# First two stages in one block with overlaid buffers; two buffers for the output weights, two groups per loop turn, exponentials head by head

## The chip, the cores and the metric

The kernel runs on one core of one Trainium2 chip. Its five engines (PE = TensorE, DVE = VectorE, ACT = ScalarE, POOL = GpSimd, SP = SyncE) run their own instruction streams and meet at semaphores. The metric is the device time of one execution, in microseconds (us).

## What is computed

Four adapter layers, each added to its input `x` (8 sequences of 128 tokens, 512 features, float32). The second is attention with 32 query heads and 8 key/value heads of size 128, rotary positions and rank-16 adapters that each sequence picks from 8.

```python
x = x + einsum('bsi,boi->bso', x, L0_weight[ids])                 # layer 0: a 512x512 weight per sequence
# layer 1, lora_linear(x, w, a, b) = x@w + (x@a[id])@b[id]
q, k = rope(lora_linear(x, wq, aq, bq)), rope(lora_linear(x, wk, ak, bk))
v    = lora_linear(x, wv, av, bv)
p    = softmax(where(causal & mask, q.k / sqrt(128), min))        # 4 query heads share a key head
x    = x + lora_linear((p @ v), wo, ao, bo)
x = x + ((x @ B[ids].T) @ A[ids].T)                               # layer 2, rank 16
x = x + x @ W.T + b + 2.0 * ((x @ lora_As[s]) @ lora_Bs[s])       # layer 3, rank 16
```

## The kernel before

Nearly every product is made of three matmuls: each float32 operand is split into a high part (rounded, by ACT) and a low part (the rest, by DVE or POOL), and PE adds hi*hi, hi*lo and lo*hi. The program is four blocks, one after the other; between two blocks all engines meet.

**Block 1** (layer 0, sequence by sequence, b = 0..7). SP loads the transposed input (256 KB), the weight of the sequence (1 MB, three buffers), `x` (256 KB) and the three `a` adapters (96 KB). ACT and DVE split them. PE makes the product (`product`, L282 to L284, 12 matmuls of 512 columns), transposes the sum with four float32 transposes (`turn_x1`, L294), multiplies by the `a` adapters (`adapters`, L306 to L308) and turns those (`turn_ax`, L318). POOL issues gathers of the `bk` and `bv` rows of the sequences into a DRAM tensor `bkv_sel` (L267, L268), from which SP later loads one block of rows with four DMAs (`load_rows`, L154).

**Block 2** (projections). 16 value units (L713 to L718: 12 matmuls of 512 columns and one for the adapters), 16 key units and 4 query units (`project`, L80 to L85), in five weight blocks. For each weight block SP loads 1 MB of weights and 1 MB of adapter rows, and ACT and DVE split them piece by piece. Value units are split and stored to DRAM by SP (L526, two DMAs for each unit, two buffers), key units are rotated by DVE and POOL and stored by SP (L531, two buffers). POOL issues gathers of `bq`, `ao`, `bo` and `l3b` rows. PE may run four units ahead of DVE (four PSUM banks).

**Block 3** (the loop). 8 groups of 4 heads, 8 slots (sequences) in each; the first and the last group are written out, the six between are a hardware loop (`over_heads`). Slot t is in order on PE: scores(t), 8 passes (L1079); queries for later (L80 to L85); turn(t-1), which transposes the probabilities as a product with an identity (L1088, L1089: eight float16 matmuls, high and low half); outputs(t-2) (L1111 to L1113, then L1120 and L1121); values(t-1) (L1097 to L1099). DVE: maxima of four heads (L1015), `ot_lo`, residual add, inverse row sums (L1032, L1034), rotation (L969, L973), `pt_lo`, `p_lo` (L1044). ACT: four exponentials (L889) after the last maximum, `pt_hi` (L872), `p_hi` (L905), `ot_hi` (L878) and the high parts of the next weights. POOL: the probabilities times the inverse sums (L944), rotation (L937), low parts of the query weights (L929). The output weights have one buffer: their high parts are made in slot 1 of their own group, two low parts by DVE (L984) and two by POOL (L954).

**Block 4** (layers 2 and 3) is not changed, but for the place of one buffer.

What sets the order around the change is the program text: each engine goes through its list in order and waits at semaphores, SP's list of DMAs included. Names and lines are in the functions below.

Of the kernel before, what the change touches and what calls it, by code (L numbers as in the profile page):

```python
# [7 lines left out]
P = 128  # L8
# [19 lines left out]
P_SCALE = 4096.0  # L28
# [3 lines left out]
def program(nc, x, xt, lora_ids, pos, attn_ids, slot_ids, mask, w0, wq, wk, wv, wo, a3, bq, bk, bv, ao, bo,  # L32
# [22 lines left out]
    bkv_sel = nc.dram_tensor("bkv_sel", (B, R, 2, KVH * D), F32, kind="Internal").ap()  # L55
# [10 lines left out]
    with whole:  # L66
# [24 lines left out]
        ident_r = sb(whole, "ident_r", [P, P], F32R)  # L91
        ident_h = sb(whole, "ident_h", [P, P], F16)
# [4 lines left out]

        row_gather = sb(whole, "row_gather", [2 * R, 2, P])

# [10 lines left out]

        attn = ExitStack()
# [3 lines left out]
        cos_t = sb(attn, "cos_t", [P, NT])  # L115
        sin_t = sb(attn, "sin_t", [P, NT])
# [4 lines left out]
        rope_cols = sb(attn, "rope_cols", [P, 3])  # L121

        blk_hi = [sb(attn, "blk_hi0", [P, KC, GW], F32R)]
        blk_lo = [sb(attn, "blk_lo0", [P, KC, GW], F32R)]
        blk_b = [sb(attn, "blk_b0", [P, PAIRS, GW], F32R)]
        VB = KVH * D // GW  # L130
        raw_w_in = sem(attn, "raw_w_in")
        raw_b_in = sem(attn, "raw_b_in")
        UNITS = B
        assert VB * GW == KVH * D and GW // D * 2 == UNITS and KC + PAIRS == UNITS

        def block_source(n):

            kind, j = ((1, n), (0, n - VB), (2, 0))[min(n // VB, 2)]
            return kind, j

        def load_block_w(dma, n):
            kind, j = block_source(n)
            dma.dma_start(raw_w[:, :, :], (wk, wv, wq)[kind][j]).then_inc(raw_w_in, 16)

        def load_block_b(dma, n):
            kind, j = block_source(n)
            cols = slice(j * GW, (j + 1) * GW)
            src = (bq_sel if kind == 2 else bkv_sel[:, :, kind, :])[:, :, cols]
            load_rows(dma, raw_b, src, raw_b_in)

        def load_rows(dma, pack, src, done):

            for quad in range(4):
                dma.dma_start(pack[32 * quad:32 * quad + 32, :, :], src.rearrange("(c two) r n -> (two r) c n", two=2)).then_inc(done, 16)  # L154


        with ExitStack() as c:
            RAW = 3
            w0_raw = [sb(c, f"w0_raw{i}", [P, KC, HID]) for i in range(RAW)]
            xt_raw = [sb(c, f"xt_raw{i}", [P, KC * T]) for i in range(RAW)]  # L160
            xt_hi = [sb(c, f"xt_hi{i}", [P, KC * T], F32R) for i in range(2)]
            xt_lo = [sb(c, f"xt_lo{i}", [P, KC * T], F32R) for i in range(2)]
            wt_hi = [sb(c, f"wt_hi{i}", [P, KC, HID], F32R) for i in range(2)]
            wt_lo = [sb(c, f"wt_lo{i}", [P, KC, HID], F32R) for i in range(2)]
            a_raw = sb(c, "a_raw", [P, B, KC, 3, R])
            a_hi = [sb(c, f"a_hi{i}", [P, KC, 3, R], F32R) for i in range(2)]
            a_lo = [sb(c, f"a_lo{i}", [P, KC, 3, R], F32R) for i in range(2)]
            axn = [sb(c, f"axn{i}", [P, 3, 4, 2, R], F32R) for i in range(2)]
            ps_y = [ps(c, f"ps_y{i}", [P, HID]) for i in range(2)]
            ps_x1 = [ps(c, f"ps_x1{i}", [P, KC, T]) for i in range(2)]  # L170
            ps_a = [ps(c, f"ps_a{i}", [P, 3, R]) for i in range(2)]
            ps_at = [ps(c, f"ps_at{i}", [P, 3, T]) for i in range(2)]
# [8 lines left out]
            gathered_kv = sem(c, "gathered_kv")  # L181
            raw_hi_done = sem(c, "raw_hi_done")
            raw_lo_done = sem(c, "raw_lo_done")
# [17 lines left out]
            axt_done = sem(c, "axt_done")  # L201

            def parts(b):
                return KC if b == 0 else 2

            def wt_parts(b, k):

                before = sum(parts(n) for n in range(b))
                return before + k * parts(b) // KC + 1

            with nc.Block() as block:
                @block.sync
                def _(sp):
                    sp.dma_start(id_rows[:, 0, :], lora_ids.rearrange("(a b) -> a b", a=1)).then_inc(lora_ids_in, 16)
                    sp.dma_start(xt_raw[0][:, :], xt[0]).then_inc(xt_in[0], 16)
                    sp.wait_ge(lora_ids_in, 16)
                    for b in range(B):
                        a = sp.value_load(id_rows[0:1, 0, b:b + 1], min_val=0, max_val=w0.shape[0] - 1)
                        if b >= RAW:

                            sp.wait_ge(wt_lo_done, wt_parts(b - RAW, KC - 1))
                            sp.wait_ge(xt_lo_done, b - RAW + 1)
                        src = w0[bass.DynSlice(a, 1)].rearrange("a p c o -> p (a c) o")
                        if b == 0:

                            for k in range(KC):
                                sp.dma_start(w0_raw[0][:, k, :], src[:, k, :]).then_inc(w0_first_in[k], 16)
                            sp.wait_ge(ids_in, 32)
                        else:
                            sp.dma_start(xt_raw[b % RAW][:, :], xt[b]).then_inc(xt_in[b % RAW], 16)  # L230
                            sp.dma_start(w0_raw[b % RAW][:, :, :], src).then_inc(w0_in[b % RAW], 16)
# [1302 lines left out]
```

## Time and profile before

| | us |
|---|---|
| median of three runs | 840.07 (839.33 to 841.19) |
| the profiled execution | 838.21, span of its instructions 836.4 |
| PE busy | 758.6 (91%) |
| DVE, ACT, POOL busy | 606.9, 360.9, 327.9 |
| mean granted clock of PE | 0.958 |
| PE's last projection starts / first scores of the loop / end of the loop | 218.54 / 225.78 / about 771 |

Busy shares are means over stages of different kinds; the stretches have to be read one by one. A matmul's duration includes its way through the array, so the distance between the starts of two is what it costs PE. Granted clock 1.0 is 2.4 GHz, 0.5 is 1.2 GHz.

### The profile page before, as it was taken

To read this page: it belongs to the slowest core of one execution; us is meant where nothing else is said; L and a number is where in the kernel's file an instruction comes from. 1 tells how busy PE (TensorE), PEld (TensorE's weight loads), DVE (VectorE), ACT (ScalarE), POOL (GpSimd) and SP (SyncE) were. 2 spreads that over 40 slices of the span, in tenths; PEclk is the share of its full clock that TensorE was granted. 3 is DMA by queue.
4 is the path that set the end of the run, shared out by engine and by line. 5 is a ranking of instruction groups with operands and counts; after the bars stand their busy time and mean duration, and the time that the engine had idled before them with its cause. 6 is when DMAs were issued, how large, how long until landed. Compare 5 with 4: busy or idle time off the path is not lost. (4 is left out here: it accounts for less than half of the span.)

```text
span 836.4 us, 13875 instructions
## 1 busy us (share of the span) xinstructions
PE 758.6 (91%) x4356; PEld 629.8 (75%) x4356; DVE 606.9 (73%) x1502; ACT 360.9 (43%) x967; POOL 327.9 (39%) x277
## 2 busy tenths in 40 slices
PE   3768849899689999999999999999999999987798
PEld 2657638687568888888888888888888888875586
DVE  3544266688488788789779778878877977854883
ACT  3545142311164464446446355446444644542550
POOL 3412620154274355337336426435524633510320
PEclk8878969999799999999999999999999999999799
DMA  8772977876205024122303303402412110610502
GB/s 296 274 225 72 281 235 190 230 244 189 65 7 170 1 64 139 39 63 67 108 17 108 113 0 97 141 0 63 138 38 63 63 38 27 136 17 4 127 17 85
DMA packets 61802, 88.92 MB, mean 106 GB/s; under 512 B 18550, under 2 KB 36118, under 8 KB 58054
## 3 DMA queue, kind: packets, MB, share of 16 engines
q1 hardware_dynamic: 59442, 81.92, 32.6%
q0 software_dynamic: 2176, 6.49, 2.6%
q8 instruction: 18, 0.29, 0.1%
q14 instruction: 18, 0.15, 0.1%
q10 hardware_dynamic: 148, 0.07, 0.0%
HBM read 73.50 MB, written 20.73 MB: 113 GB/s over the span
## 5 line engine op out<-in xcount | busy, mean ns | idle before, releaser
L944 POOL TENSOR_TENSOR prob<-prob,rinv 128x512 f32<-128x512 f32 x64 | 66.6, 1040 | 199.2 <-DVE rinv L1034 199.2
L889 ACT ACTIVATE prob<-sm,nmax 128x128 f32<-128x128 f32 x256 | 99.8, 391 | 80.3 <-DVE nmax L1015 80.3
L937 POOL TENSOR_TENSOR qt<-qc,qs 128x512 f32<-128x512 f32 x60 | 96.7, 1611 | 96.1 <-DVE qs L973 96.1
L1111 PE MATMUL ps_out<-wo_hi,ot_hi 128*128 128x512 f32 x256 | 106.4, 416 | 5.9 <-DVE ot_lo L992 3.7
L80 PE MATMUL ps_q<-x1t_hi,blk_hi 128*128 128x512 f32 x240 | 100.7, 420 | 0.0
L1113 PE MATMUL ps_out<-wo_hi,ot_lo 128*128 128x512 f32 x256 | 100.7, 393 | 0.0
L1112 PE MATMUL ps_out<-wo_lo,ot_hi 128*128 128x512 f32 x256 | 99.7, 390 | 0.0
L1015 DVE CUSTOM_DVE_ANT_0 sm<-ps_s,maskbias 128x128 f32<-128x128 f32 x256 | 58.7, 284 | 54.2 <-issue 54.1
L81 PE MATMUL ps_q<-x1t_lo,blk_hi 128*128 128x512 f32 x240 | 95.8, 399 | 0.0
L82 PE MATMUL ps_q<-x1t_hi,blk_lo 128*128 128x512 f32 x240 | 95.7, 399 | 0.0
L973 DVE TENSOR_TENSOR qs<-ps_q,sin_t 64x512 f32<-64x512 f32 x120 | 82.6, 688 | 3.7
L878 ACT ACTIVATE ot_hi<-ps_o 128x512 fp32r<-128x512 f32 x64 | 38.0, 594 | 105.6 <-PE ps_o L1099 105.4
L1079 PEld LDWEIGHTS ps_s<-kt,qt 128*128 128x128 f32 x512 | 67.6, 193 | 12.5 <-issue 7.0
L1079 PE MATMUL ps_s<-kt,qt 128*128 128x128 f32 x512 | 68.4, 277 | 6.8 <-PEq L514 6.8
L1044 DVE TENSOR_TENSOR p_lo<-prob,p_hi 128x512 f16<-128x512 f32 x64 | 59.8, 934 | 5.9 <-ACT p_hi L905 4.1
L1111 PEld LDWEIGHTS ps_out<-wo_hi,ot_hi 128*128 128x128 f32 x256 | 48.2, 188 | 15.4 <-DVE ot_lo L992 4.9
L872 ACT ACTIVATE pt_hi<-ps_t 128x512 fp32r<-128x512 f32 x64 | 38.2, 596 | 42.8 <-PE ps_t L1089 42.8
L1113 PEld LDWEIGHTS ps_out<-wo_hi,ot_lo 128*128 128x128 f32 x256 | 48.1, 188 | 11.2
L1112 PEld LDWEIGHTS ps_out<-wo_lo,ot_hi 128*128 128x128 f32 x256 | 48.4, 189 | 8.5
L82 PEld LDWEIGHTS ps_q<-x1t_hi,blk_lo 128*128 128x128 f32 x240 | 45.6, 190 | 10.9
L696 POOL TENSOR_TENSOR kr<-k_cos,k_sin 128x512 f32<-128x512 f32 x16 | 25.7, 1608 | 69.7 <-DVE k_sin L670 57.7
L905 ACT ACTIVATE p_hi<-prob 128x512 f16<-128x512 f32 x64 | 40.2, 628 | 29.1 <-POOL prob L944 28.8
(194 smaller groups left out, 1871.4 us busy)
## 6 DMA issues: line engine op xcount, KB each, us to landing
wo_raw<-in_wo SPq DMA_DIRECT2D x8, 1024.0 KB, 4.9
raw_w<-in_wq SPq DMA_DIRECT2D x8, 1024.0 KB, 5.3
w_raw<-in_w SPq DMA_DIRECT2D x7, 1024.0 KB, 9.7
raw_b<-bq_sel SPq DMA_DIRECT2D x56, 128.0 KB, 4.7
raw_b<-bkv_sel SPq DMA_DIRECT2D x16, 256.0 KB, 6.6
v_hi_d<-v_hi SPq DMA_DIRECT2D x16, 256.0 KB, 3.1
v_lo_d<-v_lo SPq DMA_DIRECT2D x16, 256.0 KB, 3.8
k_rot<-kr SPq DMA_DIRECT2D x16, 256.0 KB, 2.9
```

The costliest lines, as they stand in the source:

```text
L80: pe.matmul(bank[:, :], w_hi[:, k, cols], x1t_hi[:, k, tok], start=(k == 0), stop=False)
L81: pe.matmul(bank[:, :], w_hi[:, k, cols], x1t_lo[:, k, tok], start=False, stop=False)
L82: pe.matmul(bank[:, :], w_lo[:, k, cols], x1t_hi[:, k, tok], start=False, stop=False)
L889: e = act.activation(prob[i][:, h, :], sm[:, h, :], ACT.Exp, bias=nmax[i][:, h:h + 1], scale=-1.0, accum_out=rsum[i][:, h:h + 1])
L937: pool.tensor_tensor(qt[:, half, h, :], qc[:, :], qs[:, :], ALU.add).then_inc(q_done, 1)
L944: pool.tensor_tensor(prob[i][:, :, :], prob[i][:, :, :], rinv[i][:, :].unsqueeze(2).broadcast_to([P, G, T]), ALU.mult).then_inc(prob_done, 1)
L973: dve.tensor_tensor(qs[to:to + 64, :], ps_q[i][at:at + 64, :], sin_t[to:to + 64, tok], ALU.mult).then_inc(q_mult, 1)
L1044: dve.tensor_tensor(p_lo[:, :, :], prob[i][:, :, :], p_hi[:, :, :], ALU.subtract).then_inc(p_lo_done, 1)
L1079: mm = pe.matmul(ps_s[b % 2][:, h, :], qt[:, half, h, at:at + T], kt[:, b * T:(b + 1) * T], start=True, stop=True)
L1111: pe.matmul(ps_out[:, :], ot_hi[:, q], wo_hi[:, h, :], start=(h == 0), stop=False)
L1112: pe.matmul(ps_out[:, :], ot_hi[:, q], wo_lo[:, h, :], start=False, stop=False)
L1113: pe.matmul(ps_out[:, :], ot_lo[:, q], wo_hi[:, h, :], start=False, stop=(h == G - 1))
```

## The change

In the diff below, the loops over s are ACT's and PE's, `split_pieces` waits for all 32 DMAs of a block before the first piece of its rows, `load_a(b)` waits until the low part of the `a` adapters of sequence b-3 is made, and turn_ax(n) stands in the middle of values(n).

Blocks 1 and 2 become one block: in step s PE does value unit s-2, then product, adapters and first transposition of sequence s; key and query units follow. Most raw buffers lie over buffers that are used later. A table PIECES says in which step each quarter of a weight block is split. The gather into `bkv_sel` is gone: SP loads the adapter rows of a block directly with 32 DMAs. ACT issues the stores of the values. In the loop the float16 halves of the probabilities are gone, and PE transposes the float32 probabilities with four transposes, ahead of the queries. The output weights have two buffers and are split in slots 4 to 7 of the group before, all low parts on POOL; ACT makes each exponential after its own maximum; the loop turns three times over two groups.

```diff
+        PIECES = {1: [(0, "w", k) for k in range(KC)] + [(0, "b", 0)], 2: [(0, "b", 1)], 3: [(0, "b", 2), (0, "b", 3)],
+                  4: [(1, "b", 0), (1, "b", 1)], 5: [(1, "b", 2), (1, "b", 3)],
+                  7: [(1, "w", 0), (1, "w", 1)], 8: [(1, "w", 2), (1, "w", 3)],
+                  10: [(2, "b", 0)], 11: [(2, "w", 0)], 12: [(2, "w", 1)], 13: [(2, "w", 2)], 14: [(2, "w", 3)],
+                  15: [(2, "b", 1)], 16: [(2, "b", 2)], 17: [(2, "b", 3)]}
+        for k in range(KC):
+            PIECES[18 + k] = [(3, "w", k)]
+            PIECES[22 + k] = [(3, "b", k)]
...
+        def load_block_b(dma, j):
+            src = (bv, bv, bk, bk)[j]
+            cols = slice(j % 2 * GW, (j % 2 + 1) * GW)
+            for b in range(B):
+                pick = dma.value_load(id_rows[0:1, 1, b:b + 1], min_val=0, max_val=src.shape[0] - 1)
+                for quad in range(4):
+                    at = 32 * quad + R * (b % 2)
+                    dma.dma_start(raw_b[at:at + R, b // 2, :], src[bass.DynSlice(pick, 1), :, cols].rearrange("a r n -> (a r) n")).then_inc(raw_b_in, 16)
...
+                    load_w0(0)
+                    load_w0(1)
+                    sp.wait_ge(ids_in, 32)
+                    load_x(0)
+                    load_a(0)
+                    load_block_w(sp, 0)
+                    load_block_b(sp, 0)
+                    load_x(1)
+                    load_a(1)
+                    load_w0(2)
...
+                    for b in range(RAW, B):
+                        load_w0(b)
+                        load_x(b)
+                        load_a(b)
+                        if b == 5:
+                            sp.wait_ge(w_lo_done, KC)
+                            load_block_w(sp, 1)
+                        if b == 6:
+                            sp.wait_ge(b_lo_done, PAIRS)
+                            load_block_b(sp, 1)
...
+                    sp.wait_ge(b_lo_done, 3 * PAIRS)
+                    load_block_b(sp, 3)
+                    for m in range(VU):
+                        g, h = divmod(m, 2)
+                        sp.wait_ge(k_done, m + 1)
+                        sp.dma_start(k_rot[g, :, h * HT:(h + 1) * HT], kr[h]).then_inc(k_out[h], 16)
...
+                    for s in range(LAST):
+                        n = s - 2
+                        if 0 <= n < B:
+                            pack_hi(n)
+                        if 1 <= s <= B:
+                            split_x1(s - 1)
+                            split_a(s - 1)
+                        if s == 1:
+                            split_pieces(s)
+                        if s + 1 < B:
+                            split_xt(s + 1)
+                        if 0 <= n < B:
+                            copy_axt(n)
+                        if s + 1 < B:
+                            split_w0(s + 1, 0, KC // 2)
+                        if 0 <= n < VU:
+                            act.wait_ge(p_ready, n + 1)
+                            if n >= VR:
+                                act.wait_ge(v_out[n % VR], 32 * (n // VR))
...
+                        if s + 1 < B:
+                            split_w0(s + 1, KC // 2, KC)
+                        if s >= 2:
+                            split_pieces(s)
...
+                        if 1 <= n <= VU:
+                            store_v(n - 1)
...
+                    for s in range(LAST):
+                        if 0 <= n < VU:
+                            values(n)
...
+                            project(pe, ps_p[n % 4], wgt_hi[WGT[blk]], wgt_lo[WGT[blk]], packs[PACK[blk]], ax, head, half).then_inc(p_ready, 1)
+                        if s < B:
+                            product(s)
+                        if 1 <= s <= B:
+                            adapters(s - 1)
+                        if s < B:
+                            turn_x1(s)
...
             def over_heads(eng, slots):
-                slots(0, True, False)
-                with eng.Fori(1, KVH - 1) as g:
-                    slots(g, False, False)
+                slots(0, 0, True, False)
+                with eng.Fori(0, KVH // 2 - 1) as pair:
+                    slots(2 * pair + 1, 1, False, False)
+                    slots(2 * pair + 2, 0, False, False)
...
                             for h in range(G):
+                                act.wait_ge(max_done, G * t + h + 1)
                                 e = act.activation(prob[i][:, h, :], sm[:, h, :], ACT.Exp, bias=nmax[i][:, h:h + 1], scale=-1.0,
                                                    accum_out=rsum[i][:, h:h + 1])
...
-                            act.activation(p_hi[:, :, :], prob[i][:, :, :], ACT.Copy).then_inc(p_hi_done, 1)
+                            if first and b < 2:
+                                wo_hi_part(0, 0, 2 * b)
+                                wo_hi_part(0, 0, 2 * b + 1)
...
+                            if first and b < 2:
+                                wo_lo_part(0, 0, 2 * b)
+                                wo_lo_part(0, 0, 2 * b + 1)
                             pool.wait_ge(inv_done, t + 1)
                             pool.tensor_tensor(prob[i][:, :, :], prob[i][:, :, :], rinv[i][:, :].unsqueeze(2).broadcast_to([P, G, T]),
                                                ALU.mult).then_inc(prob_done, 1)
...
-                            dve.wait_ge(p_hi_done, t + 1)
-                            dve.tensor_tensor(p_lo[:, :, :], prob[i][:, :, :], p_hi[:, :, :], ALU.subtract).then_inc(p_lo_done, 1)
...
                     def turn(t, b):
-                        pe.wait_ge(p_lo_done, t + 1)
+                        pe.wait_ge(prob_done, t + 1)
                         if not isinstance(t, int) or t >= 1:
                             pe.wait_ge(pt_lo_done, t)
                         for h in range(G):
-                            pe.matmul(ps_t[:, h * T:(h + 1) * T], p_hi[:, h, :], ident_h[:, :], start=True, stop=False)
-                            mm = pe.matmul(ps_t[:, h * T:(h + 1) * T], p_lo[:, h, :], ident_h[:, :], start=False, stop=True)
+                            mm = pe.transpose(ps_t[:, h * T:(h + 1) * T], prob[t_parity][:, h, :], ident[:, :])
...
                             scores(t, g, b)
+                            if not first or b >= 1:
+                                turn(t - 1, (b - 1) % B)
```

## Rows read from the trace of the kernel before

**Rows 1.** The page: PE's granted clock in 40 slices of the span
```profile
PEclk8878969999799999999999999999999999999799
```
**Rows 2.** Windows: stretch, its length, busy of PE, PEld, DVE, ACT, POOL, clock, DMA share, GB/s
```profile
0.00:80.00 80.00, 50.56 (x248) 42.34 (x248) 35.23 (x48) 36.48 (x65) 23.27 (x36) 0.86 0.62 212
...
83.00:104.00 21.00, 17.58 (x73) 13.78 (x71) 5.20 (x8) 2.60 (x5) 13.49 (x23) 0.97 0.97 280
...
355.00:420.00 65.00, 64.82 (x413) 54.71 (x412) 53.59 (x147) 32.58 (x95) 31.42 (x23) 1.00 0.25 77
```
**Rows 3.** Timeline of PE: scores of slots 3, 8 and 16
```profile
250.07 1.05 PE L1079 MATMUL ps_s<-kt,qt 128*128 128x128 f32 x8
...
292.24 1.05 PE L1079 MATMUL ps_s<-kt,qt 128*128 128x128 f32 x8
...
360.04 1.05 PE L1079 MATMUL ps_s<-kt,qt 128*128 128x128 f32 x8
```
**Rows 4.** Timeline of PE, one slot: start, duration, line, tile, count
```profile
406.49 0.23 PE L1088 MATMUL ps_t<-ident_h,p_hi 128*128 128x128 f16 x1
...
406.92 0.47 PE L1111 MATMUL ps_out<-wo_hi,ot_hi 128*128 128x512 f32 x1
407.24 0.39 PE L1112 MATMUL ps_out<-wo_lo,ot_hi 128*128 128x512 f32 x1
407.46 0.40 PE L1113 MATMUL ps_out<-wo_hi,ot_lo 128*128 128x512 f32 x1
```
**Rows 5.** Timeline of PE: a value unit, the last projection, the first scores
```profile
129.91 0.39 PE L713 MATMUL ps_p<-blk_hi,x1t_hi 128*128 128x512 f32 x1
...
132.94 0.40 PE L713 MATMUL ps_p<-blk_hi,x1t_hi 128*128 128x512 f32 x1
...
218.54 0.40 PE L85 MATMUL ps_p<-axt_all,blk_b 128*128 128x256 f32 x2
...
225.78 2.05 PE L1079 MATMUL ps_s<-kt,qt 128*128 128x128 f32 x8 [6.83 <-PEq L514]
```
**Rows 6.** Timeline of PE in block 1: the first matmul, sequence 3
```profile
8.06 0.77 PE L282 MATMUL ps_y<-wt_hi,xt_hi 128*128 128x512 f32 x1 [8.06 <-DVE wt_lo L401]
...
34.41 0.50 PE L282 MATMUL ps_y<-wt_hi,xt_hi 128*128 128x512 f32 x1 [1.58 <-POOL xt_lo L248]
...
37.25 0.60 PE L294 MATMUL ps_x<-ident,res 128*128 128x128 f32 x4
37.60 0.27 PE L306 MATMUL ps_a<-a_hi,x1t_hi 128*128 128x48 f32 x1
...
38.94 0.53 PE L318 MATMUL ps_at<-ident_r,axn 128*128 128x128 f32 x3
```
**Rows 7.** Timeline of SP's queue: start, time issuing, line, tile, count
```profile
732.43 9.66 SPq L847 DMA_DIRECT2D l3a_sel<-in_l3a  x8
...
772.46 1.74 SPq L154 DMA_DIRECT2D l3b_raw<-l3b_sel  x4
```
**Rows 8.** The page's DMA issues: count, size, median us to landing
```profile
raw_w<-in_wq SPq DMA_DIRECT2D x8, 1024.0 KB, 5.3
...
k_rot<-kr SPq DMA_DIRECT2D x16, 256.0 KB, 2.9
```
**Rows 9.** Timelines of ACT, DVE and ACT in blocks 1 and 2
```profile
20.57 2.00 ACT L346 ACTIVATE wt_hi<-w_raw 128x1024 fp32r<-128x1024 f32 x2 [2.12 <-DMA w_raw<-in_w]
...
23.94 0.68 DVE L407 TENSOR_TENSOR res<-ps_y,res 128x512 f32<-128x512 f32 x1
...
108.04 0.60 ACT L583 ACTIVATE v_hi<-ps_p 128x512 fp32r<-128x512 f32 x1 [18.44 <-DMA v_lo_d<-v_lo]
```
**Rows 10.** Timelines of ACT and POOL in the first group
```profile
232.97 0.62 ACT L859 ACTIVATE blk_b<-raw_b 128x512 fp32r<-128x512 f32 x1
...
231.08 1.04 POOL L944 TENSOR_TENSOR prob<-prob,rinv 128x512 f32<-128x512 f32 x1 [8.63 <-DVE rinv L1034]
...
244.53 2.98 POOL L954 TENSOR_TENSOR wo_lo<-wo_raw,wo_hi 128x512 fp32r<-128x512 f32 x2
```

More of the change, by code:

```diff
@@ L109, in program @@
         l3a_in = sem(whole, "l3a_in")
+        with ExitStack() as ahead:
+            row_gather = sb(ahead, "row_gather", [2 * R, 2, P])
         attn = ExitStack()
@@ L131, in program @@
+        v_lo3 = sb(attn, "v_lo3", [P, B, D], F32R)
+        qt = sb(attn, "qt", [P, 2, G, HT])
         raw_w_in = sem(attn, "raw_w_in")
         raw_b_in = sem(attn, "raw_b_in")
-        UNITS = B
[L134 to L149, printed above, removed]
+        wq_in = sem(attn, "wq_in")
+        wo_in = sem(attn, "wo_in")
+        bq_in = [sem(attn, f"bq_in{i}") for i in range(2)]
+        ao_in = sem(attn, "ao_in")
+        kt_in = [sem(attn, f"kt_in{i}") for i in range(2)]
+        v_in = [sem(attn, f"v_in{i}") for i in range(2)]
@@ L319, in turn_ax @@
                                            ident_r[:, :], start=True, stop=True)
                         mm.then_inc(axt_ready, 1)
-                    for b in range(B + 3):
-                        if b < B:
-                            product(b)
-                        if 1 <= b <= B:
-                            turn_x1(b - 1)
-                        if 2 <= b <= B + 1:
-                            adapters(b - 2)
-                        if b >= 3:
-                            turn_ax(b - 3)
@@ new lines, in values @@
+                    def values(n):
+                        blk, b = divmod(n, UNITS)
+                        hi, lo, pack = wgt_hi[WGT[blk]], wgt_lo[WGT[blk]], packs[PACK[blk]]
+                        tok = slice(b * T, (b + 1) * T)
+                        o = ps_p[n % 4][:, :]
+                        for k in range(KC):
+                            if b == 0:
+                                pe.wait_ge(w_lo_done, KC * blk + k + 1)
+                            if k == KC // 2 and blk == 0:
+                                turn_ax(b)
+                            pe.matmul(o, x1t_hi[:, k, tok], hi[:, k, :], start=(k == 0), stop=False)
+                            pe.matmul(o, x1t_hi[:, k, tok], lo[:, k, :], start=False, stop=False)
+                            pe.matmul(o, x1t_lo[:, k, tok], hi[:, k, :], start=False, stop=False)
+                        if b % 2 == 0:
+                            pe.wait_ge(b_lo_done, PAIRS * blk + b // 2 + 1)
+                        if blk == 0:
+                            pe.wait_ge(axt_done, b + 1)
+                        pe.matmul(o, axt_v[:, tok], pack[:, b // 2, :], start=False, stop=True).then_inc(p_ready, 1)
@@ L914, in slots @@
                             if b == 1:
-                                wo_hi_part(g, 1)
-                                wo_hi_part(g, 3)
+                                if not first:
+                                    act.wait_ge(out_ready, B * g)
                                 ao_hi_part(g)
+                            if not last and b >= HALF:
+                                if b == HALF and not first:
+                                    act.wait_ge(out_ready, B * g)
+                                wo_hi_part(g + 1, 1 - odd, b - HALF)
                     over_heads(act, slots)
@@ L963, in _, with rotate @@
                 def _(dve):
-                    def rotate(n, half, i, before):
+                    def rotate(n, half, i):
                         tok = slice(half * HT, (half + 1) * HT)
@@ L998, in add, with slots @@
                         dve.tensor_tensor(axo[:, b, :], ps_ao[0:2 * R, 0:T], axo[:, b, :], ALU.add).then_inc(axo_done, 1)
-                    def slots(g, first, last):
+                    def slots(g, odd, first, last):
                         for b in range(B):
@@ L1122, in outputs, with slots @@
                         mm.then_inc(out_ready, 1)
-                    def slots(g, first, last):
+                    def slots(g, odd, first, last):
                         for b in range(B):
@@ L1127, in slots @@
                             scores(t, g, b)
+                            if not first or b >= 1:
+                                turn(t - 1, (b - 1) % B)
                             if b < HALF:
```

955 lines of the change are left out of this document (442 added, 513 removed).

## The prediction

> **What bounds the kernel now.** I read the windows first, then the timelines at their borders. In the loop PE is busy 64.82 of 65 us at clock 1.00 with DMA at a quarter [rows 2]: nothing but less work on PE shortens a slot. The scores of slots 3 and 8 start 42.17 us apart, 8.43 a slot, and slots 8 and 16 are 67.80 apart, 0.34 more than eight slots: the price of a turn of the hardware loop [rows 3]. Inside a slot the queries end and the turn starts at 406.49, the outputs start at 406.92: eight float16 matmuls take 0.43. The first output matmul takes 0.32 until the next, that one 0.22: 0.09 for coming from small tiles [rows 4].
>
> Ahead of the loop it is otherwise. PE's last projection starts at 218.54, so PE ends at 218.8; it then stands 6.83 us at the border and starts the loop at 225.78, where eight passes take 2.05 us against 1.05 later, on the lower of the two clocks [rows 3, 5]. The same shows in the clock digits of the first ten slices, 6 to 9 [rows 1]. In the first 80 us PE has only 50.56 busy [rows 2]. What must it do there at full clock? A value unit is 3.03 (129.91 to 132.94) [rows 5]; I take 3.04 for key and query units, which have as many columns. A product is 2.84, four float32 transposes 0.35, adapters 1.34 [rows 6], `turn_ax` like the transposes, 0.35. Sum: 8 x 4.88 + 16 x 3.03 + 20 x 3.04 = 148.3. With the first product at 8.06 as now [rows 6], an unbroken block would end at 156.4; 62.4 of the 218.8 are waits and low clock. That is what a merged block can win, at most.
>
> **The merged block.** The question is what it waits for instead. The new thing is `load_block_b`: 8 value loads and 32 DMAs of 32 KB in SP's queue, four times. No row shows such a DMA. A value load and a DMA are 9.66/8 = 1.21 us, and a further DMA 1.74/4 = 0.43 though its shape is regular [rows 7]. I take 0.5 for a further one, since each computes its address: 8 x (1.21 + 3 x 0.5) = 21.7, so T = 22 us. Bounds: 8 x (1.21 + 3 x 0.3) = 17 if 16 rows issue quicker, 8 x (1.21 + 3 x 0.7) = 26 if the address costs more. The first begins at about 9, once the first weights and the small loads are issued.
>
> Step by step: *(a) Start.* x(1), a(1) and w0(2) are behind block 0 in SP's list; with 9 + 22 and two value loads and four DMAs more, w0(2) is issued at about 34.5. A megabyte lands 5.3 after its issue [rows 8]: 39.8. From the start of such a split to the end of the add behind it takes 24.62 - 20.57 = 4.05 [rows 9], and `add(1)` stands behind `split_w0(2)` on DVE, with `turn_x1(1)` behind it on PE: step 2 begins at 44.2. Done by then: two products, two transpositions, one set of adapters, 7.7. Lost: 44.2 - 8.1 - 7.7 = 28.4. Step 2 runs partly at the low clock: 2.6 (a dozen matmuls at twice their 0.22, [rows 3 to 5]). Steps 2 and 3 then take about 10 and 8 us: step 4 at 62.
> *(b) Step 4.* Block 1 of the rows is behind a(6), which waits for the split of a(3) in step 4: issue begins 2.7 into the step, ends T later, lands 2.9 after that (a key store's time, [rows 8]). ACT's pieces of step 4 wait for all 32; behind them on ACT stands the whole of step 5, and PE needs its `pack_hi(3)` for the second half of values(3). It resumes 2.7 + 22 + 2.9 + 2.7 (two pieces, two stores, the pack on ACT and DVE) = 30.3 into the step and has work for 8.0 + 1.4: lost 20.9, and 2.5 at the low clock.
> *(c) Values.* Steps 8 to 17 carry 5 MB of value stores, 4 MB of gathers and 1 MB of weights in 30 us. The window where gathers and stores meet now has DMA at 0.97 and 280 GB/s [rows 2], by which 10.4 MB need 37 us; and a store kept `v_hi` waiting 18.44 there [rows 9]. Three buffers and spread gathers help. Between 0 and 18 I take 8.
> *(d) Keys.* SP stands in block 3 of the rows, T long, from the end of the values on; the first key store leaves 24 us late. PE has eight units (four banks, two buffers, two in DVE), 24.3 us, then waits for the stores (2.9 to landing [rows 8]), POOL, DVE and the pieces of steps 22 to 25: I follow these to 7.7 at the second block and 2.5 one unit later, 10.2; 1.5 more for the last block. Bounds 3 and 16.
> Lost in all: 28.4 + 2.6 + 20.9 + 2.5 + 8 + 10.2 + 1.5 = 74.1, against 62.4. The merged block ends **12 us later**. Each us of T counts about three times, in (a), (b) and (d).
>
> **The loop.** Four float32 transposes, which before the adapters take 0.35 for 0.43, and the outputs no longer come behind small tiles, 0.09 [rows 4, 6]: 0.17 at most a slot; I take 0.15 for 60 slots, **-9**. Bounds: -11, and 0, if the transposes wait for their loads behind the scores. Three turns for six: **-1** (3 x 0.34). The DVE and ACT work that goes (`p_lo`, `p_hi`) lies beside PE's and is worth nothing; nor are earlier exponentials, as `pt_hi` is now ahead of them. turn(t-1) stands 3 us earlier, but the probabilities are ready some 6.3 us after the scores of their slot (231.08 + 1.04 - 225.78, [rows 5, 10]), 2.9 ahead of it: no wait where a slot has queries.
>
> In slots 0 and 1 it is different: POOL makes two low parts of wo *ahead* of the probabilities, and these wait for ACT, behind its query split. ACT's `bq` part ends at 232.97 + 0.62, 7.8 after the loop's start [rows 5, 10]; one high part of 0.6, two low parts in 2.98 and the 1.04 of the multiply [rows 10] bring the probabilities of slot 0 at 12.4. turn(0), now ahead of queries(1), stands since about 7.3 (two sets of scores and a query unit, in part at the low clock). It is followed by a low clock (1.7) and a second wait of 3.8 in slot 2. The scores of slot 3 come at 31.6 rather than at 250.07 - 225.78 = 24.3 [rows 3]: **+7** (3 to 9). The last group has shorter chains: **-1**. Layers 2 and 3, and their loads, finish ahead of the loop's end as now.
>
> A rule weighed. Four transposes cost PE 0.35 where they stand now, 0.09 each [rows 6]. The Trainium skill ("TensorE: Matmul & The Clock Gate", PE-mode transpose) says that a transpose of 128x128 was measured at about 275 ns inside a kernel. The row's 0.60 for four is of that kind, with the way through the array in it, and the next matmul starts after 0.35. Were 275 ns the price, a slot's turn would be 1.1 for 0.43 and the loop 0.67 x 64 = 43 us longer.
>
> Sum: +12 - 9 - 1 + 7 - 1 = +8 on the profiled execution's own 838.21 (its span is 836.4): 846. The median of the runs, 840.07, stands 1.9 above that execution: **848**.
>
> **Rivals.**
> *R1, the merge pays.* Value loads and DMAs of 16 rows issue at T = 17 or less, and the stores fall between the gathers (c at 2). Three times 5, and 6, are 21 less: 827; at T = 14, 818. For it: the stalls of now (a store wait of 18.4) have gone, SP has no gather to wait for. Against: 128 issues at 0.43 are 55 us alone. It decides below T of about 20 with (c) at 6, where 3 x 2 + 2 take up the 8.
> *R2, the other side of the same: ACT as store queue.* It issues two stores a unit in order; a full queue holds it, and with it `v_hi` and the splits. With (c) at 18 and T at 26 it is 10 + 12 more than the forecast: 870. For it: the 18.44. Against: three buffers.
> *R3, the loop gives nothing.* Transposes behind scores cost what the halves cost: +9, 857. A transpose that holds PE as long as 0.28 each would give 848 + 9 + 43 = 900.
> *R4, the waits are hidden*, because PE, ACT and DVE catch up from step 6 on better than my chain says: so that PE is done near 156 + 35 = 191 and not 231: 808.
>
> **How the numbers follow.** Less than 0.2% (1.7 us) can't be told from no change here. My forecast (838 to 860) 0.45; R1 0.28; R2 0.11; R3 0.05 and its last case 0.02; R4 0.09. Faster is R1 and R4, 0.37, less 0.01 for their part of the band; within 0.2% is the forecast's lowest part, 0.08; slower the rest, 0.56. Range: from R4's edge to R2, 809 to 870; the forecast's own is 838 to 860.
>
> **What would show it.** Right: SP issuing for about 22 us for each block of rows; PE idle until about 44 but for two products, and again some 20 us in the fifth step; PE's last projection near 230; turns of 0.35 and slots of 8.28 in the loop; PE idle 5 us ahead of the first turn. Wrong: a block of rows issued in less than 18 us; no ACT wait for rows in step 4; the loop starting before 226.

## The result, and the profile after

The changed kernel takes **863.43 us** (median of 4 runs, 861.25 to 865.41) where the kernel before, beside it, took 839.82 (839.33 to 841.19): ratio 1.0278, 95% interval 1.0245 to 1.031. The forecast was 848, within a range of 809 to 870: the direction and the range held, the size didn't; the change costs 23.6 us and not 8.

The profiled execution took 865.41 us with a span of 863.7, so 27.3 more than the span of before (836.4). The two profiled executions lie 2.0 above and 1.6 below their medians, which is why the traces differ by more than the 23.6 of the times. I split the 27.3 at the scores of slots 0 and 8 [rows 3, 5] and of slot 56:

| stretch | before | after | difference | forecast |
|---|---|---|---|---|
| up to the loop's first scores | 225.78 | 239.21 | +13.4 | +12 |
| group 0 | 66.46 | 73.47 | +7.0 | +7, less 1 for its slots |
| groups 1 to 6 | 406.85 | 416.95 | **+10.1** | about -8 |
| group 7 and what follows | 137.3 | 134.1 | -3.2 | -2 |

Slot 56 opens group 7, in the kernel before and in the changed one:

```profile
699.09 1.05 PE L1079 MATMUL ps_s<-kt,qt 128*128 128x128 f32 x8
```

```profile
729.63 1.16 PE L1093 MATMUL ps_s<-kt,qt 128*128 128x128 f32 x8
```

One line of four is wrong, and by its sign. The page of the changed kernel: busy time, PE's granted clock in 40 slices, and the queues that carry instructions (packets, MB, share).

```profile
span 863.7 us, 13575 instructions
PE 759.9 (88%) x4100; PEld 628.7 (73%) x4100; DVE 515.9 (60%) x1354; ACT 320.3 (37%) x902; POOL 311.7 (36%) x281
PEclk8597899989979999999999999999999999999799
q8 instruction: 39, 0.64, 0.3%
q14 instruction: 33, 0.27, 0.1%
```

The page of before has the same two queues, with about half the packets:

```profile
q8 instruction: 18, 0.29, 0.1%
q14 instruction: 18, 0.15, 0.1%
```

DVE is busy 91 us less than before and ACT 41, and the loop got no shorter by it: PE bounds the loop.

**The merged block.** The steps are numbered from 0, and each engine goes through them at its own pace. SP's queue (start, time issuing, line, tiles, count), and the three longest pauses of PE behind it (in brackets the idle time before the row, and its releaser):

```profile
9.77 19.33 SPq L177 DMA_DIRECT2D raw_b<-in_bv  x32
...
63.67 19.05 SPq L177 DMA_DIRECT2D raw_b<-in_bv  x32
...
96.23 20.97 SPq L177 DMA_DIRECT2D raw_b<-in_bk  x32
...
156.22 20.67 SPq L177 DMA_DIRECT2D raw_b<-in_bk  x32
```

```profile
41.63 0.69 PE L695 MATMUL ps_x<-ident,res 128*128 128x128 f32 x2 [16.97 <-DVE res L499]
...
86.44 0.90 PE L718 MATMUL ps_ax<-ident_r,axn 128*128 128x128 f32 x3 [17.04 <-DVE axn L509]
...
183.95 0.76 PE L78 MATMUL ps_p<-x1t_hi,wgt_hi 128*128 128x512 f32 x1 [5.87 <-DVE pack L521]
```

The second row, in the middle of PE's values(3), names DVE, but DVE had been waiting too. ACT's rows show what ended it. ACT stands in its step 4 for 19.04 us until the rows are there, and makes the pack that PE wants (the second row, `pack_hi(3)`) only behind them.

```profile
84.14 0.63 ACT L432 ACTIVATE pack<-raw_b 128x512 fp32r<-128x512 f32 x1 [19.04 <-DMA raw_b<-in_bv]
...
85.22 0.25 ACT L411 ACTIVATE axn<-ps_ax 128x96 fp32r<-128x96 f32 x1
```

**The loop.** PE's timeline: the scores of slot 0, the first two turns, the scores that open groups 1 to 6, and on either side of the first jump back those of the last slot of group 2 and of the second slot of group 3.

```profile
239.21 2.05 PE L1093 MATMUL ps_s<-kt,qt 128*128 128x128 f32 x8 [6.84 <-PEq L288]
...
251.09 1.06 PE L1102 MATMUL ps_t<-ident,prob 128*128 128x128 f32 x4 [4.43 <-POOL prob L982]
...
261.16 0.91 PE L1102 MATMUL ps_t<-ident,prob 128*128 128x128 f32 x4 [3.22 <-POOL prob L982]
...
312.68 1.15 PE L1093 MATMUL ps_s<-kt,qt 128*128 128x128 f32 x8
...
380.40 1.15 PE L1093 MATMUL ps_s<-kt,qt 128*128 128x128 f32 x8
...
439.48 1.05 PE L1093 MATMUL ps_s<-kt,qt 128*128 128x128 f32 x8
...
452.27 1.80 PE L1093 MATMUL ps_s<-kt,qt 128*128 128x128 f32 x8 [4.24 <-issue]
...
462.36 1.05 PE L1093 MATMUL ps_s<-kt,qt 128*128 128x128 f32 x8
...
521.62 1.15 PE L1093 MATMUL ps_s<-kt,qt 128*128 128x128 f32 x8
...
592.86 2.07 PE L1093 MATMUL ps_s<-kt,qt 128*128 128x128 f32 x8 [3.59 <-issue]
...
662.07 1.15 PE L1093 MATMUL ps_s<-kt,qt 128*128 128x128 f32 x8
```

Groups 1, 3 and 5 lead to the next in 67.72, 69.35 and 69.21; groups 2 and 4 take 71.87 and 71.24. The doubled body holds groups 1 and 2, then 3 and 4, then 5 and 6: its two jumps back are ahead of 452.27 and 592.86. PE stands there 4.24 and 3.59 us for nothing that the profile shows ("issue"), and then runs scores in 1.80 and 2.07 instead of 1.05, on the lower of the two clocks. Going by slots, the one ahead of the jump is 12.79 and 12.15, the one behind it 10.09 and 9.96; in the run with PE's loop written out (experiment 3) each of these is 8.49 or 8.50. That makes 11.0 us for the two jumps. The traces of experiments 5, 8 and 9, which keep the doubled body, show the same two places, with 12.2 to 12.9 and 9.8 to 10.1.

### The profile page after: what moved, and what is told of

Read it like the earlier page. It is cut to its first block and busy times, and to the rows that moved or that the text cites. A ratio compares the mean times of both kernels' runs of the same rounds, so it can differ in the third digit from the quotient of the medians.

```text
span 863.7 us, 13575 instructions
## 1 busy us (share of the span) xinstructions
PE 759.9 (88%) x4100; PEld 628.7 (73%) x4100; DVE 515.9 (60%) x1354; ACT 320.3 (37%) x902; POOL 311.7 (36%) x281
## 5 line engine op out<-in xcount | busy, mean ns | idle before, releaser
L1122 PE MATMUL ps_out<-wo_hi,axt_all 128*128 128x512 f32 x256 | 101.7, 397 | 4.3 <-DVE axt_all L1019 2.4
L78 PE MATMUL ps_q<-x1t_hi,wgt_hi 128*128 128x512 f32 x240 | 102.3, 426 | 0.0
L1123 PE MATMUL ps_out<-wo_lo,axt_all 128*128 128x512 f32 x256 | 101.3, 396 | 0.0
L1124 PE MATMUL ps_out<-wo_hi,axt_all 128*128 128x512 f32 x256 | 100.8, 394 | 0.0
L80 PE MATMUL ps_q<-x1t_hi,wgt_lo 128*128 128x512 f32 x240 | 96.5, 402 | 0.0
L79 PE MATMUL ps_q<-x1t_lo,wgt_hi 128*128 128x512 f32 x240 | 96.5, 402 | 0.0
L1004 DVE TENSOR_TENSOR qs<-ps_q,trig 64x512 f32<-64x512 f32 x120 | 82.6, 689 | 3.7
L1122 PEld LDWEIGHTS ps_out<-wo_hi,axt_all 128*128 128x128 f32 x256 | 48.3, 188 | 14.8 <-DVE axt_all L1019 4.0
L1124 PEld LDWEIGHTS ps_out<-wo_hi,axt_all 128*128 128x128 f32 x256 | 48.0, 187 | 11.6
L1123 PEld LDWEIGHTS ps_out<-wo_lo,axt_all 128*128 128x128 f32 x256 | 48.2, 188 | 8.5
L80 PEld LDWEIGHTS ps_q<-x1t_hi,wgt_lo 128*128 128x128 f32 x240 | 46.2, 193 | 11.1
L78 PEld LDWEIGHTS ps_q<-x1t_hi,wgt_hi 128*128 128x128 f32 x240 | 47.1, 196 | 8.3
```

What stands on the lines that cost most here:

```text
L78: pe.matmul(bank[:, :], w_hi[:, k, cols], x1t_hi[:, k, tok], start=(k == 0), stop=False)
L79: pe.matmul(bank[:, :], w_hi[:, k, cols], x1t_lo[:, k, tok], start=False, stop=False)
L80: pe.matmul(bank[:, :], w_lo[:, k, cols], x1t_hi[:, k, tok], start=False, stop=False)
L1004: dve.tensor_tensor(qs[to:to + 64, :], ps_q[i][at:at + 64, :], sin_t[to:to + 64, tok], ALU.mult).then_inc(q_mult, 1)
L1122: pe.matmul(ps_out[:, :], ot_hi[:, q], wo_hi[odd][:, h, :], start=(h == 0), stop=False)
L1123: pe.matmul(ps_out[:, :], ot_hi[:, q], wo_lo[odd][:, h, :], start=False, stop=False)
```

## The experiments

Times are medians; where a run is set against the changed kernel, that is its 863.43. Each ratio is to runs of the kernel before on the same chip (838.7 to 840.66), so a difference of 2 us between two versions is no more than what the chips differ by.

**1. The doubled body alone, in the kernel before.**

```diff
-                with eng.Fori(1, KVH - 1) as g:
-                    slots(g, False, False)
+                with eng.Fori(0, KVH // 2 - 1) as pair:
+                    slots(2 * pair + 1, False, False)
+                    slots(2 * pair + 2, False, False)
```

> The kernel before, and in it only the loop's body doubled on PE, ACT, DVE and POOL: two groups of heads per turn of the hardware loop, three turns for six. Theory J (what the new kernel's loop lost is the jump back of a doubled body, whose instructions are read in anew): PE stands about 4 us at each of the two jumps back and then runs scores at the lower clock for about 1.5 us, so 2 x 5.5 = 11 us more, less 3 x 0.34 for the turns saved: 850 us. Rival W (the pauses come from something the change waits for, the two buffers of the output weights or the transposes' new place): 839, one us less than before, for three turns of 0.34 saved.

Measured: 849.44 us, ratio 1.0104 [1.0051, 1.0157]: 8.8 more. No buffer, transpose or order differs from the kernel before. The pauses are in its timeline where theory J puts them, at the openings of groups 3 and 5:

```profile
434.16 2.07 PE L1080 MATMUL ps_s<-kt,qt 128*128 128x128 f32 x8 [2.78 <-issue]
...
574.48 2.07 PE L1080 MATMUL ps_s<-kt,qt 128*128 128x128 f32 x8 [3.01 <-issue]
```

Rival W is out: the price comes with the doubled body alone.

**2. The changed kernel, the middle groups written out on all four engines.** `with eng.Fori(...) as pair` becomes `for pair in range(KVH // 2 - 1)`.

> The changed kernel, its loop over the middle six groups written out, no hardware loop on PE, ACT, DVE and POOL; the order of the work is untouched. Theory J: both pauses of some 5.5 us go, but all instructions have now to come in once, which they can do ahead of their use: 863.4 - 11 = 852 us. Rival W (a semaphore's wait, which is the same in the written-out code): 863. A second rival, R: the code, eight groups long, is read in too slowly wherever it is new, so that pauses come in every group: above 863.

Measured: 850.85 us, 1.0118 [1.006, 1.0177]: 12.6 less than the changed kernel. The groups stand 67.5 apart throughout, so rival W has nothing left here either, and rival R is refuted.

**3. The same on PE alone**; ACT, DVE and POOL keep their doubled body.

> The changed kernel with the loop over the middle groups written out on PE alone; ACT, DVE and POOL keep their hardware loop of two groups. Theory P (it is PE's own instructions that come late after the jump back, 12.79 and 12.15 us instead of 8.67 between two slots): as in the wholly written-out kernel, 863.4 - 12 = 851 us, and all group starts 67.5 apart. Rival O (another engine's jump back is what PE stood for, unseen because its branch is not a busy row): 859 to 863.

Measured: 849.81 us, 1.0121 [1.008, 1.0162]: 13.6 less, 67.53 from group to group with no pause anywhere: theory P holds, and rival O is out. The two slots at the place of the first pause, for 12.79 above:

```profile
437.12 1.05 PE L1098 MATMUL ps_s<-kt,qt 128*128 128x128 f32 x8
...
445.61 1.16 PE L1098 MATMUL ps_s<-kt,qt 128*128 128x128 f32 x8
```

It is PE's own jump back that costs. Of the 13.6, 11.0 are the slots at the two jumps. About 1 us more comes in small pieces: in the changed kernel the fourth slot of each middle group is 8.56 and the eighth slot of groups 0, 1, 3 and 5 is 8.67, and written out they are 8.49 or 8.50. The rest is within the spread of the runs.

Here q8 still brings 3 or 4 packets in each 70 us of the loop, and PE never stands. In the kernel before, neither queue moves anything from 370 to 650 us. That the pause is the time to read in the start of a body that is no longer held after a jump fits both pages. No row shows an instruction missing, and no run makes the body long in another way, so this stays an inference. The place (PE's jump back) and the price are shown.

**4. The kernel before, PE's middle groups written out.** It tells what an undisturbed group of before costs.

> The kernel before, with the loop over its six middle groups written out on PE alone. The prediction read the 67.80 between groups, 0.34 over eight slots of 8.43, as the price of a turn of the hardware loop. Theory J0 (as the prediction says): the 0.34 sits at the jump and goes, six times: 2 us less, group starts 67.45 apart. Theory V (it sits in the slot from the fourth to the fifth scores, 8.80 for 8.43, in every group and also in the doubled body, where PE works out a register's value ahead of a wait): as much goes, 2 us, but from the fourth slot, and the step from the eighth slot to the next group stays 8.43. Theory N (it is neither: the fourth slot's wait for the values' load or the low parts): no change, 840.

Measured: 838.8 us, 1.0002 [0.9972, 1.0031]: no difference, and 1.7 us in 839 could hardly be seen in the times. The traces are finer. These are the fourth and the eighth slot of group 2 (each is the distance between the two rows), first in the kernel before, then written out:

```profile
385.34 1.05 PE L1079 MATMUL ps_s<-kt,qt 128*128 128x128 f32 x8
...
394.14 1.05 PE L1079 MATMUL ps_s<-kt,qt 128*128 128x128 f32 x8
...
419.43 1.05 PE L1079 MATMUL ps_s<-kt,qt 128*128 128x128 f32 x8
...
427.86 1.05 PE L1079 MATMUL ps_s<-kt,qt 128*128 128x128 f32 x8
```

```profile
386.02 1.05 PE L1084 MATMUL ps_s<-kt,qt 128*128 128x128 f32 x8
...
394.45 1.05 PE L1084 MATMUL ps_s<-kt,qt 128*128 128x128 f32 x8
...
419.75 1.05 PE L1084 MATMUL ps_s<-kt,qt 128*128 128x128 f32 x8
...
428.19 1.05 PE L1084 MATMUL ps_s<-kt,qt 128*128 128x128 f32 x8
```

In the kernel before the fourth slot of each of groups 1 to 6 is 8.80 and the eighth 8.43. Written out, the fourth is 8.43 from group 2 on, and the groups stand 67.47 apart. So the 0.34 never sat at the jump, though most of it goes with the loop. Group 1 keeps its 8.80 although nothing there is worked out from a register any more: theory V has the place right, and its cause is not confirmed.

**5. The rows of the adapters without their price.** `load_block_b` is replaced by `load_rows(dma, raw_b, src[0:B, :, cols], raw_b_in)`.

> The changed kernel, with each block of 32 adapter DMAs and 8 value loads replaced by four DMAs of 64 to 256 KB out of the first eight adapters (left out: the pick of the adapter by its id). Theory T (SP's 19 to 21 us for each block of rows stand behind the pauses of the merged block): the pauses of 17.0 before step 2 and 17.0 in step 4, and most of the key phase's 12, shrink to 5 together; about 35 us less than the changed kernel, 828 us. Rival C (the merged block waits for memory traffic and for chains through ACT and DVE, rows or no rows): under 12 us less, 852 or more.

Measured: 830.44 us, 0.9881 [0.9832, 0.993]: 33.0 less than the changed kernel, so theory T holds in size and rival C is out. The loop's first scores come at 207.02 instead of 239.21. The pause of step 4 is 3.9, but that before step 2 is still 10.4, where the theory wanted 5 for the two.

**6 and 7. One block of rows at a time**: the same replacement under `if j == 0`, then under `if j == 1`.

> The changed kernel, with block 0 of the rows alone loaded by four DMAs out of the first eight adapters (left out: the pick of the adapter in that block); blocks 1 to 3 as changed. The prediction's chain (a), w0(2) is issued T later and all behind it moves by as much: 17 us less, 846. Rival A (the pause before step 2 shrinks only from 17.0 to the 10.4 that it has in the run with all rows plain, and part of this comes back as a longer pause in step 4, because block 1 is then waited for sooner): 5 to 8 us less, 855 to 858.

> The changed kernel, with block 1 of the rows alone loaded by four DMAs out of the first eight adapters (left out: the pick in that block). The prediction's chain (b), ACT stands in step 4 for the 32nd DMA of this block: the pause of 17.0 goes, less 3 that stay: 14 to 16 us less with the low clock behind it, 848. Rival L (the loads of w0 and the adapters' factors behind it in the queue were as late, so that the next wait takes its place): 5 us less or under, 858 or more.

Measured: block 0, 855.59 us, 1.0195 [1.0152, 1.0239], 7.8 less; block 1, 849.55 us, 1.0129 [1.0086, 1.0171], 13.9 less. In the first the pause before step 2 falls from 17.0 to 8.0, and that of step 4 stays at 17.2. The prediction's 17 us less is refuted, and the transfer of w0(2) shows why. The rows are its issue on SP and the split on ACT that waits for it, first in the changed kernel, then in experiment 6:

```profile
31.82 0.34 SPq L312 DMA_DIRECT2D trig<-in_w  x1
...
37.53 2.00 ACT L393 ACTIVATE wgt_hi<-trig 128x1024 fp32r<-128x1024 f32 x2 [3.16 <-DMA trig<-in_w]
```

```profile
13.98 0.35 SPq L315 DMA_DIRECT2D trig<-in_w  x1
...
28.31 2.01 ACT L396 ACTIVATE wgt_hi<-trig 128x1024 fp32r<-128x1024 f32 x2 [2.62 <-DMA trig<-in_w]
```

It is issued 17.8 us sooner and used only 9.2 sooner, since now all the first loads stand in line together: from 14 to 28 us the DMA share is 1.05 at 301 GB/s, where the changed kernel has 0.38 and 121. Rival A has the size, though not its reason, as nothing came back in step 4. In the second run the pause of step 4 falls from 17.0 to 4.3, as expected. Of the 33.0, 21.7 are these two. The other 11.3 are put down to the key blocks' rows by subtraction; no run took these alone.

**8. The rows gathered by POOL.** POOL copies each request's rows of `bv`, later of `bk`, into a buffer in DRAM, and SP loads a block with four DMAs; all is computed.

```diff
+                    for b in range(B):
+                        gather_kv(1, b)
...
-            for b in range(B):
-                pick = dma.value_load(id_rows[0:1, 1, b:b + 1], min_val=0, max_val=src.shape[0] - 1)
-                for quad in range(4):
...
+            load_rows(dma, raw_b, bkv_sel[:, :, 1 - j // 2, cols], raw_b_in)
```

> The changed kernel, with the adapters' rows gathered by POOL into a buffer in DRAM (8 + 8 DMAs, 0.95 us each with its value load by the kernel before's rows) and each block of rows loaded from it by four DMAs on SP, the first behind x(1) and a(1). Unlike the run with plain rows it computes everything. Theory T (SP's 19 to 21 us of issue were the whole cost): within 5 us of the run with plain rows, 830 to 835 us. Rival G (POOL's gathers, which start near 6 us and end near 14, hold up xt_lo and a_lo, and the first rows land at about 20): 838 to 845.

Measured: 837.72 us, 0.9967 [0.9946, 0.9988]: 25.7 less than the changed kernel, and 7 more than with plain rows. It falls just under rival G's range, and what G says is in the trace: POOL's eight gathers run from 6.09 to 14.43, 1.1 us each, and SP can issue the first rows only at 18.55.

**9. POOL's order in the first group**: `wo_lo_part(0, 0, ...)` goes behind the probabilities and `rotate`.

> The changed kernel, with POOL's two low parts of wo in slots 0 and 1 put behind the probabilities and the rotation of their slot instead of ahead of them. Theory O (the prediction's: in the first group the probabilities wait behind these parts, and these behind ACT): the waits of 4.4 and 3.2 ahead of turn(0) and turn(1) go, slot 3 starts 24.3 after the loop's start instead of 31.0: 7 us less, 856. Rival E (the probabilities wait for the exponentials anyway): 2 us less or none, 861 to 863.

Measured: 857.11 us, 1.0203 [1.0152, 1.0253]: 6.3 less. Group 0 is 67.22 instead of 73.47; turn(0) no longer waits, and a wait of 2.81 ahead of turn(1) is left. Theory O holds.

**10. The transposes back behind the queries.**

```diff
-                            if not first or b >= 1:
-                                turn(t - 1, (b - 1) % B)
                             if b < HALF:
                                 queries(t, 1, b, None if first else (G * g, PAIRS * g))
                             elif not last:
                                 queries(t, 0, b - HALF, (G * g + b - HALF + 1, PAIRS * g + 2))
+                            if not first or b >= 1:
+                                turn(t - 1, (b - 1) % B)
```

> The changed kernel, with the four float32 transposes put back behind the query unit, where the kernel before has its float16 ones; all else as changed. Theory S (behind the scores the first transpose costs 0.08 us more, as scores 0.81 to 0.89 show, and ahead of the outputs they would cost 0.35 and no more): the slots get 0.05 to 0.1 us shorter, and the 8 us of waits for the probabilities in slots 1 and 2 go: 5 to 12 us less than the changed kernel, 851 to 858. Rival P (what is late sets the end: with the transposes 3 us later their split on ACT comes behind the exponentials' start and the values wait): 863 or more.

Measured: 897.13 us, 1.0668 [1.0612, 1.0724], 34 us *more* than the changed kernel. Theory S fails in the sum. It is right that the waits of slots 1 and 2 go (the first three slots take 24.9 us instead of 31.0), but undisturbed slots are 8.37 to 8.38 for 8.38 to 8.39, not 0.05 to 0.1 shorter, and at most half groups the slot ahead of the new half and the first slot in it each grow by 1.5 to 2 us. Rival P has the direction, not the place: the values don't wait, the next half's scores do. The chain across POOL, ACT and DVE ahead of slot 4 of group 1:

```profile
339.12 0.60 PE L1102 MATMUL ps_t<-ident,prob 128*128 128x128 f32 x4
...
339.76 0.60 ACT L903 ACTIVATE axt_all<-ps_t 128x512 fp32r<-128x512 f32 x1 [3.77 <-PE ps_t L1102]
...
341.93 0.18 DVE L1058 RECIPROCAL rinv<-rsum 128x4 f32<-128x4 f32 x1
...
344.22 1.26 POOL L963 TENSOR_TENSOR qt<-qc,qs 128x512 f32<-128x512 f32 x1 [0.99 <-DVE qs L1004]
...
345.61 1.83 PE L1093 MATMUL ps_s<-kt,qt 128*128 128x128 f32 x8 [1.89 <-POOL qt L963]
```

The program has ACT split the transposed probabilities ahead of the exponentials. With the transposes 3 us later, ACT, free for 3.77, holds the exponentials back with them; the reciprocal follows, DVE's rotation stands behind the reciprocal and POOL's sum of it behind that, and the scores of a new half need that sum. That is read from the order of these rows. It says that the early place of the transposes is a condition of ACT's new order, not a gain by itself.

**11. Every transpose twice**, in the changed kernel with PE's loop written out: `for h in (*range(G), *range(G))`.

> The changed kernel with PE's loop written out (849.8 us), and in it each slot's four float32 transposes made twice, into the same places. Theory S (the rows: the next matmul starts 0.35 after four of them): 64 x 0.30 to 0.35 = 19 to 22 us more, 869 to 872. Rival D (about 275 ns each, the Trainium skill's figure in TensorE: Matmul & The Clock Gate, PE-mode transpose, were the price of one in a row): 64 x 1.1 = 70 more, 920. Rival Z (they lie in PE's slack): none more, 850.

Measured: 876.32 us, 1.0433 [1.0382, 1.0484], 26.5 more than 849.81: 0.41 for four, 0.10 each. The slots grow from 8.39 and 8.49 to 8.83. That is theory S, at 4 us above its range; rivals D and Z are out. The Trainium skill has about 275 ns for one 128x128 transpose inside a kernel ("TensorE: Matmul & The Clock Gate", PE-mode transpose). The mean duration of one in this run is the same, 275 ns, but a duration is not what one in a row costs:

```profile
L1107 PE MATMUL ps_t<-ident,prob 128*128 128x128 f32 x512 | 67.2, 275 | 7.7 <-POOL prob L987 7.7
```

**12. The three repairs together** (8, 9 and PE's loop written out).

> Three edits together on the changed kernel: rows gathered by POOL and loaded in four DMAs, the loop over the middle groups written out on PE alone, POOL's low parts of wo behind the probabilities. If the three causes are apart: 837.7 - 12 - 7 = 819 us, 2.5% under the kernel before. If they overlap (a group that starts sooner meets loads that are as late as before): 825 or more.

Measured: 816.75 us, 0.9724 [0.9676, 0.9773]. The single gains, 25.7 + 6.3 + 13.6 = 45.6, give 817.8: they add up, so the three causes are apart.

**13. And DVE's first two adds ahead of the split of the next weights.**

```diff
+                        if s < 2:
+                            add(s)
                         if s + 1 < B:
                             split_w0(s + 1, 0, KC // 2)
```

> The three edits of the best version, and DVE's add of the first two products ahead of the split of the next weights, which waits for their load. Theory Q (turn_x1(0) and turn_x1(1) stand 5.5 and 9.2 us behind an add that waits for weights it does not need): PE does the transposes, adapters and splits of step 1 in these pauses, 2 to 4 us less than without. Rival W0 (the next product needs those weights anyway, and all that comes before it is short): under 1 us.

Measured: **812.25 us, 0.9665 [0.9617, 0.9714]**, 3.4% under the kernel before and 4.5 us under the version without. The pauses ahead of the first two `turn_x1` fall from 6.15 and 9.54 to 2.84 and 7.05, and the loop starts at 204.99 instead of 210.98. Theory Q holds, and the gain is a little more than it said.

## Why the prediction was wrong, point by point

- **T = 22, three waits.** Measured 19.3, 19.1, 21.0 and 20.7 in the order of issue. Right in kind, 1 to 3 us high.
- **(a)** Step 2 begins at 41.6 (said: 44.2). Right. That each us of T counts there in full is wrong: 17 us less gave 7.8 (experiment 6), as w0(2) then waits for the other transfers.
- **(b)** PE idle 17.0 in the middle of values(3), ended by ACT's wait for the rows (said: 20.9). Right, mechanism and place.
- **(c)** 8 for the values' traffic: too much. From 86.44 to the end of the values PE waits 1.51 and 1.31; DMA is at 0.73 from 104 to 134, in the middle of the values, where before it stood at 0.97 [rows 2]. Behind that it does rise to 1.04 and 322 GB/s, and PE is busy 15.49 us of 16 all the same, so full DMA engines alone don't stop PE there (columns as in [rows 2]):

```profile
104.00:134.00 30.00, 27.18 (x135) 22.13 (x134) 17.54 (x24) 12.05 (x22) 9.26 (x13) 1.00 0.73 222
134.00:150.00 16.00, 15.49 (x67) 12.18 (x66) 15.60 (x16) 5.64 (x10) 8.30 (x9) 1.00 1.04 322
```

- **(d)** 11.7 for the keys: too little. The pauses are 4.73, 5.87, 1.67, 1.06, 3.15 and 0.92, 17.4 in all. (c) and (d) nearly cancel. (a) and (b) were together 6 too high, and what takes this up is a term that the sum put at nothing: the low clock behind the keys' pauses. From 155 to 159, 184 to 189 and 217 to 220 the matmuls start 0.43 apart instead of 0.23, by my estimate 5.5 us in all. So the 13.4 for the 12 said is in part errors that cancel.
- **Group 0, +7.** Measured 7.0, by the waits named (4.43 and 3.22), and experiment 9 takes 6.3 of it back.
- **"Three turns for six: -1 (3 x 0.34)" is the step that failed most.** It read eight slots of 8.43 and a group of 67.80, and put the difference at the hardware loop's jump without looking at where in the group it lay. It lies in the fourth slot (experiment 4), and the jump of the body of one group costs nothing that the trace shows: the eighth slot, with the jump in it, is 8.43. From that false price it took fewer jumps as a gain, as if a jump's price did not depend on the body. The body of two groups pays 5.5 us at each of two jumps: +11 for -1. The 11 are nearly half of the change's whole cost.
- **"I take 0.15 for 60 slots, -9" failed too.** With PE's loop written out the groups are 67.47 in the kernel before (experiment 4) and 67.53 in the changed one (experiment 3): nothing gained. In the loops as they are, a group is 67.80 in the kernel before and 67.72 in the changed one where no jump of the doubled body touches it (group 1). The step had two halves. Four slots in eight gain 0.05: the turn is 0.36 for 0.43 and the outputs 2.80 for 2.85, but the scores ahead of the transposes take 0.89 for 0.81, the cost that the forecast's bound of 0 named. The other four, two at each half group, lose about 0.06. In the first of the two this is a wait that I had not seen: PE's weight load of the scores stands for POOL's rotation, which ends at 411.79. In the second the scores take 1.00 until the next matmul instead of 0.89; why is not shown. Rival R3 (the loop gives nothing, 857) was right on the sum of the slots, at a chance of 0.05, and only in part for its reason.

Three rows of experiment 3 show that wait, in brackets. No run took it away, so its share is read and not tested:

```profile
410.49 1.30 POOL L968 TENSOR_TENSOR qt<-qc,qs 128x512 f32<-128x512 f32 x1 [0.98 <-DVE qs L1009]
...
411.84 0.97 PEld L1098 LDWEIGHTS ps_s<-kt,qt 128*128 128x128 f32 x8 [0.38 <-POOL qt L968]
...
411.84 1.16 PE L1098 MATMUL ps_s<-kt,qt 128*128 128x128 f32 x8
```

Put in the forecast's sum, the jumps (+11 for -1) and the slots (0 for -9) make +8 into +29 on the spans, where 27.3 were measured. The parts of the front, the first group and the end are each within 2 of what was said. R1 and R4, the cases of a gain, had 0.37 between them. Neither came, but experiment 8 shows R1's condition at work: with a cheap way to the rows the merged block is worth its waits.

## What to carry to other kernels

A doubled body of a hardware loop is an edit with a price of its own: look at the profile's instruction queues and at the slots around the jump on the bounding engine, and write that engine's loop out if they are longer than the others. When a group is longer than its slots, find the slot that is longer before giving the difference a name. Of a block of small, computed DMAs, ask which engine's whole order stands behind the last one, and have an idle queue gather them.

## What the runs showed that was not expected

- Four engines ran the doubled body, and the price was PE's alone; written out there, 4 us of standing and a spell at the lower clock went at each jump (ratio 1.0278 to 1.0121).
- A pause of about 3 to 4 us costs some 1.5 more behind it: scores at 1.80 to 2.07 for 1.05, and a slot of 10.0 for 8.49. Behind the second pause of experiment 1 it was more, a slot of 11.31 for 8.43.
- Moving four transposes, 0.36 us together, by 3 us cost 34 us. The rows put it down to the order on ACT, which is busy 35% of the time.
